# Half of the first chunk loaded ahead of the first weight matrix and the condition, in a gated residual kernel

## What is computed

```
h    = silu(cond @ W1.T + b1)
gate = sigmoid(h @ W2.T + b2)[:, None, :]
# pairwise sums and differences over N, all scaled by gate, then inverted
return x + (v + a)          # v = x
```

## Time and profile before

| | |
|---|---|
| median of 3 runs | 166.62 us |
| profiled execution, its own time | 166.82 us |
| its span (first to last instruction) | 165.1 us |
| outside the span | 1.72 us |
| moved by DMA | 69.47 MB, mean 421 GB/s |
| VectorE busy | 80.0 us (48%), 20 instructions |
| TensorE busy | 22.7 us (14%), 68 instructions |
| ScalarE, GpSimd busy | 2.5 us, 2.6 us |

### The profile page before, as it was taken

The page is one execution under the profiler, slowest core; times in us unless marked ns, Lnnn a source line. Parts: engine busy times, 40 slices in busy tenths (PEclk is TensorE's granted clock), DMA queues, the critical chain, the costliest instruction groups (busy, mean ns, idle before and its releaser), DMA issues.

```text
span 165.1 us, 219 instructions
## 1 busy us (share of the span) xinstructions
PE 22.7 (14%) x68; PEld 12.2 (7%) x68; DVE 80.0 (48%) x20; ACT 2.5 (2%) x3; POOL 2.6 (2%) x10
## 2 busy tenths in 40 slices
PE   0099969800000000000000000000000000000000
PEld 0093722300000000000000000000000000000000
DVE  0052380499999999999970000000004999700000
ACT  3000100100000000000000000000000000000000
POOL 6000000000000000000000000000000000000000
PEclk9999987995555555555555555555555555555555
DMA  5999969969998997989997996999899799799995
GB/s 151 474 456 508 476 286 508 508 286 476 508 397 365 508 508 254 508 349 413 508 429 334 508 508 302 461 508 413 349 508 445 334 492 508 318 445 405 445 421 254
DMA packets 1732, 69.47 MB, mean 421 GB/s; under 512 B 194, under 2 KB 194, under 8 KB 324
## 3 DMA queue, kind: packets, MB, share of 16 engines
q1 hardware_dynamic: 1008, 43.25, 61.4%
q10 hardware_dynamic: 724, 26.22, 36.9%
HBM read 35.92 MB, written 33.55 MB: 421 GB/s over the span
## 4 chain that ended last, share of the span: by engine, by line
DMA 50%; DVE 19%; PE 12%; DVEq 5%; ACT 1%; issue 0%
DMA ring<-in_x 23%; DMA out<-ring 22%; DVE ring L242 10%; DVE ring L247 5%; DVEq L30 5%; DMA ring<-in_L_cond_W 5%; PE gate_sum L173 3%; PE turned L181 2%; PE hidden_sum L151 2%; PE turned L135 2%; DVE ring L229 2%; PE hidden_sum L146 1%; PE turned_cond L140 1%; DVE factor L237 0%; DVE ring L222 0%; ACT ring L193 0%
## 5 line engine op out<-in xcount | busy, mean ns | idle before, releaser
L242 DVE TENSOR_TENSOR ring<-ring,factor 128x16384 f32<-128x16384 f32 x3 | 51.5, 17220 | 0.0
L247 DVE TENSOR_TENSOR ring<-ring,factor 128x8192 f32<-128x8192 f32 x2 | 17.3, 8688 | 40.5 <-DMA ring<-in_x 40.5
L216 DVE COPY ring<-turned 128x512 f32<-128x512 f32 x4 | 2.8, 692 | 10.0 <-PE turned L135 10.0
L237 DVE TENSOR_SCALAR factor<-turned 128x512 f32<-128x512 f32 x4 | 2.8, 691 | 6.9 <-PE turned L181 6.9
L173 PE MATMUL gate_sum<-ring 128*128 128x512 f32 x8 | 5.4, 833 | 1.3 <-DVE ring L227 1.3
L135 PE MATMUL turned<-identity,ring 128*128 128x128 f32 x16 | 3.6, 423 | 8.4 <-DMA ring<-in_L_cond_W 8.4
L229 DVE COPY ring<-turned 128x512 f32<-128x512 f32 x4 | 3.9, 1056 | 0.0
L135 PEld LDWEIGHTS turned<-identity,ring 128*128 128x128 f32 x16 | 3.3, 227 | 8.4 <-issue 8.4
L181 PE MATMUL turned<-ring 128*128 128x512 f32 x8 | 3.7, 601 | 0.8 <-ACT ring L193 0.8
L151 PE MATMUL hidden_sum<-ring 128*128 128x512 f32 x8 | 3.7, 605 | 0.0
L222 DVE TENSOR_TENSOR ring<-hidden_sum,ring 128x512 f32<-128x512 f32 x1 | 0.7, 692 | 5.6 <-ACT ring L190 5.6
(11 more groups left out here) (17 smaller groups left out, 6.6 us busy)
## 6 DMA issues: line engine op xcount, KB each, us to landing
out<-ring ACTq DMA_DIRECT2D x2, 4096.0 KB, 20.8
ring<-in_L_cond_W ACTq DMA_DIRECT2D x1, 1024.0 KB, 7.7
ring<-in_L_cond_W SPq DMA_DIRECT2D x1, 1024.0 KB, 7.5
ring<-in_cond SPq DMA_DIRECT2D x1, 256.0 KB, 7.7
ring<-in_x SPq DMA_DIRECT2D x3, 34.6
b_row<-in_L_cond_b ACTq DMA_DIRECT2D x2, 2.0 KB
out<-ring SPq DMA_DIRECT2D x2, 45.6
ring<-in_x ACTq DMA_DIRECT2D x1, 38.6
```

Of the source, the lines that this page charges most:

```text
L216: dve.tensor_copy(w1_t[:, c, :], turned[c][:, :]).then_inc(w1_t_set, 1)
L242: dve.tensor_tensor(ring[:, c, :, :], ring[:, c, :, :], steps_of(c, STEPS), ALU.mult).then_inc(chunk_scaled, 1)
L247: dve.tensor_tensor(ring[:, 0, piece(h), :], ring[:, 0, piece(h), :], steps_of(CHUNKS - 1, PIECE), ALU.mult).then_inc(chunk_scaled, 1)
```

## The change

SP issues steps 0 to 15 of chunk 0 first, then W1, then the condition, then steps 16 to 31 of chunk 0, then chunk 1. That is one DMA instruction more. Both halves count up the same semaphore, and VectorE waits for both (32 instead of 16) before it multiplies chunk 0, which it still does in one instruction. The constant is renamed, since it serves both places.

```diff
--- before.py
+++ after.py
@@ -11,7 +11,7 @@
 STEPS = 32
 GROUPS = 4
 SLOTS = 3
-LAST_PIECES = 2
+PIECES = 2
 DMA_DONE = 16
 
 
@@ -19,7 +19,7 @@
     B, N, D = x.shape
     BLOCKS = D // P
     CHUNKS = N // STEPS
-    PIECE = STEPS // LAST_PIECES
+    PIECE = STEPS // PIECES
     PER_GROUP = CHUNKS // GROUPS
     assert B == P and D == BLOCKS * P and CHUNKS == SLOTS + 1 and N == CHUNKS * STEPS and GROUPS * PER_GROUP == CHUNKS
 
@@ -78,7 +78,7 @@
         chunk_loaded = [sem(f"chunk_loaded{c}") for c in range(CHUNKS)]
         chunk_scaled = sem("chunk_scaled")
         chunk_stored = [sem(f"chunk_stored{c}") for c in range(CHUNKS)]
-        last_stored = [sem(f"last_stored{h}") for h in range(1, LAST_PIECES)]
+        last_stored = [sem(f"last_stored{h}") for h in range(1, PIECES)]
 
         block = ctx.enter_context(nc.Block())
 
@@ -94,9 +94,12 @@
 
         @block.sync
         def _(sp):
+
+            sp.dma_start(ring[:, 0, piece(0), :], chunk(x_parts, 0)[:, piece(0), :]).then_inc(chunk_loaded[0], DMA_DONE)
             sp.dma_start(w1_rows, w1.rearrange("(p t) k -> p t k", t=BLOCKS)).then_inc(w1_loaded, DMA_DONE)
             sp.dma_start(cond_rows, cond).then_inc(cond_loaded, DMA_DONE)
-            for c in range(SCRATCH):
+            sp.dma_start(ring[:, 0, piece(1), :], chunk(x_parts, 0)[:, piece(1), :]).then_inc(chunk_loaded[0], DMA_DONE)
+            for c in range(1, SCRATCH):
                 sp.dma_start(ring[:, c, :, :], chunk(x_parts, c)).then_inc(chunk_loaded[c], DMA_DONE)
 
 
@@ -199,14 +202,14 @@
             act.dma_start(chunk(out_parts, SLOTS - 1), ring[:, SLOTS - 1, :, :]).then_inc(chunk_stored[SLOTS - 1], DMA_DONE)
 
             done = [chunk_stored[CHUNKS - 1]] + last_stored
-            for h in range(LAST_PIECES):
+            for h in range(PIECES):
                 act.wait_ge(chunk_scaled, CHUNKS + h)
                 act.dma_start(chunk(out_parts, CHUNKS - 1)[:, piece(h), :],
                               ring[:, 0, piece(h), :]).then_inc(done[h], DMA_DONE)
 
             for c in range(CHUNKS):
                 act.wait_ge(chunk_stored[c], DMA_DONE)
-            for h in range(1, LAST_PIECES):
+            for h in range(1, PIECES):
                 act.wait_ge(last_stored[h - 1], DMA_DONE)
 
         @block.vector
@@ -238,12 +241,12 @@
             dve.wait_ge(factor_set, GROUPS)
 
             for c in range(CHUNKS - 1):
-                dve.wait_ge(chunk_loaded[c], DMA_DONE)
+                dve.wait_ge(chunk_loaded[c], (PIECES if c == 0 else 1) * DMA_DONE)
                 dve.tensor_tensor(ring[:, c, :, :], ring[:, c, :, :], steps_of(c, STEPS),
                                   ALU.mult).then_inc(chunk_scaled, 1)
 
             dve.wait_ge(chunk_loaded[CHUNKS - 1], DMA_DONE)
-            for h in range(LAST_PIECES):
+            for h in range(PIECES):
                 dve.tensor_tensor(ring[:, 0, piece(h), :], ring[:, 0, piece(h), :], steps_of(CHUNKS - 1, PIECE),
                                   ALU.mult).then_inc(chunk_scaled, 1)
```

## The result

The changed kernel takes 167.84 us, the median of 15 runs (166.80 to 168.82), against 166.67 us for the kernel before beside it (15 runs, 166.52 to 167.25). The ratio is 1.0056 (95% interval 1.0041 to 1.0071): slower by some 0.9 us; the medians alone are 1.2 us apart. The changed kernel's runs are also spread over 2 us, where those of before lie within 0.7. The profiled execution took 167.93 us.

What follows compares the result with a forecast made beforehand. Bound by moving 69.47 MB, with transfers filling 162.3 of 165.1 us; zero for stream, added transfer and start on the profiled 166.82 us, which was 0.20 above the median, gave 166.6 us, range 166.2 to 167.1.

Steps and rivals of the forecast that it cites:

- The added transfer and the order: One DMA transfer more, half of chunk 0 ahead of W1: taken as costing nothing, 0.7 us as the upper end.
- The stores of chunks 0 and 1 come before their turn: SP's queue: stores issued at 60.9 and 78.1 us, their turns at 67.8 and 87.3, so no cost.
- VectorE's wait before chunk 3: VectorE's wait before line 247: claimed to shrink from 40.3 to 30.6 us.
- the stream's start: First 8 us of loads: about 2 us of stream lost; taken as unchanged, with rival C (faster) at chance 0.10.
- either of the two values I had weighed: W2's landing on ACT's queue beside the half chunk: near 8 or near 14 us, both before its use.
- the slack of chunk 2's load: SP's issue of chunk 2, at 42.9 us: could come 2.2 to 4.8 us later without cost; was 11.9.
- the last safe moment: Latest issue of chunk 2 before the queue empties: 45.1 us, if 2.6 us for starting and landing must fit before 47.7.
- the slip: Chain behind W1, line 135 to the factor: 9.7 us later, chunk 2's issue moving from 33.2 to 42.9 us.
- rival A: Slower: chain slips too far, TensorE's clock included, SP's queue runs dry at 47 us; 168.1 to 176 us, chance 0.04.
- the 421 ns as a slow start: TensorE's first transposes, line 135: 421 ns against 283 on line 160, read as the engine starting throttled.
- each microsecond of further delay costs a microsecond: Chunk 2's issue: without the cover left of chunk 1's transfer, further delay costs the stream its full length.
- the rival at 168.8: Rival B at a higher price: added transfer pays the skill page's fixed 2.0 us in the stream; B's chance 0.03.

Runs made afterwards that it cites:

- the second measurement: The changed kernel itself run again, nothing altered, against the kernel before: 167.32 us, ratio 1.0027.
- 8 steps ahead of W1: Changed kernel with 8 steps of chunk 0 loaded ahead of W1 and 24 behind, against the kernel before: 166.71 us, ratio 0.9999.
- 24 steps: Changed kernel with 24 steps of chunk 0 loaded ahead of W1 and 8 behind, against the kernel before: 171.77 us, ratio 1.0295.
- the kernel with 17 memsets: Kernel before with only SP's issue of chunk 2 held back by 17 GpSimd memsets behind the last gate_spread: 167.66 us, ratio 1.0043.
- 14 steps ahead: Changed kernel with 14 steps of chunk 0 loaded ahead of W1 and 18 behind, against the kernel before: 167.11 us, ratio 1.0018.
- the kernel before with chunk 2 cut: Kernel before with chunk 2 loaded as 6 steps right behind chunk 1 and 26 behind gate_spread: 167.26 us, ratio 1.0025.
- two passes more: Kernel before with two further VectorE passes over chunk 2, each a multiplication by 1.0: 166.82 us, ratio 1.0006.
- 16 memsets: Kernel before with TensorE's first transpose, and so the whole chain, held back by 16 GpSimd memsets behind W1's landing: 167.14 us, ratio 1.0027.
- the kernels with 14, 17 and 20 of them: Kernel before with only SP's issue of chunk 2 held back by 14, 17 or 20 GpSimd memsets: 166.70, 167.66 and 168.33 us.

## Why the prediction was wrong

It gave 166.6 us (166.2 to 167.1) and "same" at 0.80. Measured were 167.84 and, in the second measurement, 167.32, both above the range.

**What held.** The stream of bytes sets the time. W1 lands at 17.95 for 18.0. The added transfer and the order cost at most 0.2 us: with 8 steps ahead of W1 the time is 166.71 (ratio 0.9999, up to 1.0014). The stores of chunks 0 and 1 come before their turn, and VectorE's wait before chunk 3 shrank to 31.0 us for 30.6. Nothing was won at the stream's start: the first packets start between 1.8 and 1.9 us in both kernels, and chunk 0 lands at 28.3 in both. W2 landed at 15.6 us, later than either of the two values I had weighed, and still before its use at 29.0.

**The step that failed** is the slack of chunk 2's load, "2.2 us at least, and up to 4.8", with 45.1 as the last safe moment. Two numbers in it were wrong, and in the same direction.

First, the slip. I took the chain as a block that moves by 9.7 us: 42.9. The profile shows 10.5: 43.7. I had the clock as rival A and put its decision at a whole stage at the lower level; the 1.7 us more of line 154 (0.3 and 0.4 of it won back on lines 138 and 143) were enough. A's mechanism came about with a further slip of 0.8 us, where I had it decide from 2.2 us on, and it had a chance of 0.04. My reading of the 421 ns as a slow start is weaker than I made it, too: the granted clock reads 1.00 in the kernel before all through 8 to 13 us, where the slow transposes are, so only their durations speak for it.

Second, the edge. I took the landing of chunk 1, 47.7, less 2.6 us for starting and landing. But a landing is the end of a transfer on its slowest engine, and the engines had started their last packets by then, from 44.3 to 44.9 us in the kernel before. A new issue needs 1.0 us to become packets (0.8 to 1.8 at the start of the kernel; 49.4 to behind 50.2 with 24 steps). By the length of the first packets of chunk 2, no engine was late at 42.9 and 43.4, none in one profile at 43.7 and two in another, six at 44.5. So the last safe moment is around 43.5 (an estimate: 44.3 to 44.9 less 1.0), not 45.1; my 42.9 was just before it, and the changed kernel is on both sides of it. That an engine must hold its next packet before it starts its last one fits these counts, but I didn't test it by itself; at 43.7 fourteen of sixteen got away with it.

And I thought of the queue as one: full or dry, with "each microsecond of further delay costs a microsecond". Between full and dry stand 16 engines. Two late ones cost 0.9 us at once, and nothing that the other fourteen do makes up for it. That would make the large spread of runs: each execution has its own clock pattern, so its own issue, and its own number of engines caught. It is argued from a profile or two of each kernel; the engines of the other executions weren't seen.

One of the prediction's numbers is off without any effect: the rival at 168.8 adds 2.0 us to the profiled 166.82; on the median, on which the forecast stands, it would be 168.6.

**What is not settled.** In the stage from 87 us on, a load and a store at once, some executions lose up to 1.8 us: 14 steps ahead (39.3 for 38.6), 24 steps ahead (40.4), and also the kernel before with chunk 2 cut (39.5) and with two passes more (39.1), where nothing was late. VectorE's work beside it doesn't show as the cause. In the changed kernel's first profile it is 0.3 of the 1.1 us (38.9 for 38.6), with 14 steps ahead all of it. What starts it stays open, and with it what the medians of 14 steps (167.11) and of 16 memsets (167.14) owe to the edge: in their profiles no engine was caught. So is why the two measurements of the changed kernel differ by 0.5 us, beyond their clocks, and why the last packets of chunk 2 took longer in the kernel with 17 memsets.

## What to carry to other kernels

In this kernel, bound by a stream of transfers, the slack of a late issue was not "landing of the one before less its latency". The measure that fits is the start of the last packets on the earliest engine (44.3 us), less the time from issue to first packet (1.0 us); keep what the chain may vary by (2.8 us below) as reserve. Windows shorter than a packet, in GB/s, count engines, but the edge of a window can cut off two of them by chance, as 49.75 did. So read the DMA share beside the GB/s: a share that is high for its GB/s means packets that take longer. With packets after the old end it shows an engine left behind where the 40 slices show a full stream. When a change widens the spread of runs, look for a wait that is won or lost by a margin smaller than the jitter of what feeds it.

## What the runs showed that I had not expected

In the changed kernel's first profile TensorE's granted clock fell from 1.00 to 0.50 at 24.4 us while TensorE was busy in every window from 18.1 us on. From 21.8 to 23.8 us it ran line 149, matmuls of one partition x 128, then the first of line 154. Whether line 149 has to do with it isn't shown: its like in the kernel before, line 146 from 12.9 to 15.0 us, brought no fall. In the kernel before, the fall at 23.4 us came behind a stretch of near idleness. The Trainium skill (TensorE: Matmul & The Clock Gate, the clock gate) ties the throttle to how busy the engine has been; here time busy did not prevent it.

The chain's length varies with that clock in the kernel before too, where nothing shows it: the memsets that wait for the last `gate_spread` start at 33.1, 34.7 and 35.9 us in the kernels with 14, 17 and 20 of them, whose chains are the same. The kernel before has 10 us of slack over that jitter of 2.8 us, the changed kernel none.
